# Pairs of row tiles: layer 0's second addition at the pair's end, residues of the four sums on VectorE, residues of the weight differences on GpSimd

## The reference

```
x = x + einsum('bnr,bor->bno', einsum('bni,bri->bnr', x, B[ids0]), A[ids0])
base   = x @ W.T
logits = x @ Wr.T + 5.0 * one_hot(ids1)
gates  = softmax over the top 2 of logits, spread over 8 experts
h      = x @ A1 (8 experts x rank 16)
x = x + base + 2.0 * einsum('bter,bte,eor->bto', h, gates, B1)
```

## Time and profile before

| | us |
|---|---|
| median of 3 runs | 607.76 (602.59 to 610.08) |
| the profiled execution | 612.9 |
| its span, first to last instruction | 611.1 |
| TensorE matmuls busy | 542.6 (89%) |
| VectorE busy | 436.6 (71%) |
| GpSimd busy | 286.4 (47%) |
| ScalarE busy | 273.9 (45%) |
| mean granted TensorE clock, as a share of full | 0.944 |

### The profile page before, as it was taken

One profiled execution on the slowest core, in us unless ns is written; L12 is line 12 of the kernel. 1 busy time (PEld: TensorE's weight loads), 2 busy tenths in 40 slices (PEclk: granted clock), 3 DMA queues, 4 the chain that ended last, 5 costly groups with the idle time before them and its releaser, 6 DMA issues.

```text
span 611.1 us, 9805 instructions
## 1 busy us (share of the span) xinstructions
PE 542.6 (89%) x3356; PEld 479.2 (78%) x3356; DVE 436.6 (71%) x904; ACT 273.9 (45%) x617; POOL 286.4 (47%) x263
## 2 busy tenths in 40 slices
PE   6899999988977889988788897979889798897997
...
GB/s 341 237 103 123 113 112 113 113 113 31 126 69 86 83 107 55 121 86 139 77 66 115 55 139 86 105 95 60 105 86 125 96 39 113 79 103 1 2 92 47
DMA packets 31158, 60.45 MB, mean 99 GB/s; under 512 B 4348, under 2 KB 20476, under 8 KB 31108
## 3 DMA queue, kind: packets, MB, share of 16 engines
...
...
## 4 chain that ended last, share of the span: by engine, by line
PE 42%; DVE 32%; issue 11%; ACT 7%; POOL 5%; DMA 1%; DVEq 1%; POOLq 0%; ACTq 0%
PE o_bank L728 14%; PE o_bank L691 8%; PE x_bank L737 8%; DVE a_raw L1306 5%; PE x_bank L610 5%; DVE weight L1376 4%; DVE xt L1229 3%; DVE xt L1256 3%; ACT bx_pair L934 3%; DVE gate L1380 2%; DVE gate L1383 2%; POOL xs L519 2%; POOL xt L525 2%; PE o_bank L680 2%; DVE b_raw L1298 2%
## 5 line engine op out<-in xcount | busy, mean ns | idle before, releaser
L728 PE MATMUL o_bank<-w_hi,xs 128*128 128x512 f32 x384 | 134.8, 424 | 5.5 <-ACT out_sb L1039 5.3
L536 POOL TENSOR_TENSOR a_t<-a_raw,a_t 64x1024 fp32r<-64x1024 f32 x22 | 52.6, 2389 | 180.2 <-ACT a_t L907 164.0
L728 PEld LDWEIGHTS o_bank<-w_hi,xs 128*128 128x128 f32 x384 | 78.6, 205 | 26.4 <-ACT out_sb L1039 8.7
L691 PE MATMUL o_bank<-w_hi,xs 128*128 128x324 f32 (+1 forms) x336 | 93.5, 352 | 0.0
L728 PE MATMUL o_bank<-w_lo,xs 128*128 128x512 f32 x192 | 80.1, 417 | 0.0
L519 POOL TENSOR_TENSOR xs<-xt,xs 128x512 fp32r<-128x512 f32 x48 | 61.7, 1297 | 38.1 <-ACT xs L991 25.0
L399 POOL DMA_INDIRECT a_in<-in_L_cond_A_dram,a_run x64 | 60.9, 952 | 19.0 <-issue 16.2
L691 PEld LDWEIGHTS o_bank<-w_hi,xs 128*128 128x128 f32 x336 | 62.2, 196 | 5.5 <-issue 1.0
L1306 DVE STREAM_TRANSPOSE a_raw<-a_in 128x1024 f32<-128x1024 f32 x32 | 64.1, 2005 | 3.0 <-DMA a_in<-in_L_cond_A_dram,a_run 3.0
L1184 DVE TENSOR_TENSOR xs<-x_bank,xs 128x512 fp32r<-128x512 f32 x64 | 43.1, 684 | 27.9 <-ACT xt L973 27.4
L1229 DVE STREAM_TRANSPOSE xt<-x_near 128x512 f32<-128x512 f32 x48 | 54.4, 1154 | 9.3 <-POOL xt L525 9.3
...
## 6 DMA issues: line engine op xcount, KB each, us to landing
...
a_in<-in_L_cond_A_dram,a_run POOLq DMA_INDIRECT x64, 3.5
...
```

Source lines behind the costliest of these rows:

```text
L536: nc.gpsimd.tensor_tensor(lower, a_raw[Q:P, m % 2, :], lower.bitcast(F32), ALU.subtract)\
L691: mm = pe.matmul(O[part][:, 0:hi - lo], x1_at(n, c // CB, low)[:, c % CB, :], w[:, c, lo:hi], start=(k == 0), stop=(k == K3 - 1), skip_gro ...
L728: mm = pe.matmul(O[0][:, 0:hi - lo], xs[:, raw_slot(j, c // CB), low, c % CB, :], w[:, c, lo:hi], start=(k == 0), stop=(k == K3 - 1), skip ...
```

## The change

- TensorE: `add_l0(b + 2)` goes from between B2 and `turn_gated` b to the very end of the pair, behind lora b. `make_bx(a + 2)` goes behind lora a, `add_l0(a + 2)` and `make_bx(b + 2)` behind `pair_first_part` b. `turn_gated` a waits for tile a's counts alone.
- VectorE gets the residues of S1 to S4 (`s_lo`) and S4's addition (`make_s4`), which goes to a buffer `s4` of its own, so S2 and the transposes need not wait for each other in the old way. `sums_of_pair` moves from a pair's end to the next pair's start, and the transposes of the next x are spread over the pair in halves.
- GpSimd keeps, in the pairs, A's residue and the gathers. The first `a_lo_paired` waits for the gates of tile a (`gate_step`), the second for the end of a + 2's fold (`bx_step`), and all six gathers come after both. In the single tiles it takes the residues of the weight differences from VectorE (`t_chunk_lo`, m = 6 to 9).
- ScalarE's order follows. Its `t_split` goes one single tile earlier (n = 3 to 6), and the split of b's result goes to the start of the next pair.

```diff
             for m in range(3, K + 2):
...
+                if m >= 6:
+                    t_chunk_lo(m - 6)
+                    pool.wait_ge(t_lo, 2 * (m - 5))
...
             for q in range(PAIRS):
                 a = K + 2 * q
-                s_lo(q, S3, s3_slot(q), xt[:, 0, chunks(0), :])
-                s_lo(q, S2, s2_slot(q), xt[:, 1, chunks(1), :])
-                make_s4(q)
-                if a + 2 < T:
-                    pool.wait_ge(s4_made, q + 1)
-                    a_lo_paired(a + 2, a + 3, a + 3)
-                s_lo(q, S1, s1_slot(q), xt[:, 1, chunks(0), :])
-                s_lo(q, S4, s4_slot(q), xt[:, 1, chunks(1), :])
+                pool.wait_ge(gate_step, GATE * (a + 1))
...
+                if a + 2 < T:
+                    if q == 0:
+                        pool.wait_ge(f_lo, CB)
+                    a_lo_paired(a + 2, a + 3, a + 3)
+                    pool.wait_ge(bx_step, bx_count(a + 3))
+                    a_lo_paired(a + 3, a + 3, a + 3)
                 if a + 4 < T:
                     reload_b(a + 4)
+                    reload_a(a + 4)
                     reload_b(a + 5)
-                    reload_a(a + 4)
-                if a + 2 < T:
-                    pool.wait_ge(ss_lo, 4 * q + S4)
...
-                    a_lo_paired(a + 3, min(a + 5, T - 1), min(a + 4, T - 1))
-                if a + 4 < T:
                     reload_a(a + 5)
...
                 pair_lora(a, 0, O[0])
                 pair_lora(a, 1, PA)
                 if more:
+                    make_bx(a + 2)
+                pair_first_part(q, 1)
+                if more:
+                    add_l0(a + 2)
                     make_bx(b + 2)
-                    add_l0(a + 2)
-                pair_first_part(q, 1)
...
                 product(B2, *w_block(0, 1), PB, False)
-                if more:
-                    add_l0(b + 2)
                 turn_gated(b, bx_count(b + 2) + 1 if more else bx_count(T))
...
                 pair_lora(a, 2, PC)
+                if more:
+                    add_l0(b + 2)
...
-                if K - CB <= n < K:
-                    t_split(n - (K - CB))
+                if 3 <= n < 3 + CB:
+                    t_split(n - 3)
                 out_part(n, 2)
...
+            def make_s4(q):
+                dve.wait_ge(s_step, 3 * q + 3)
+                if q > 0:
+                    dve.wait_ge(ss_lo, 4 * q)
+                nc.vector.tensor_tensor(s4[:, :, :], xt[:, 0, chunks(1), :], xt[:, 1, chunks(1), :],
+                                        ALU.subtract).then_inc(s4_made, 1)
+
+            def s_lo(q, which, slot, raw):
+                dve.wait_ge(ss_hi, 4 * q + which)
+                minus(xs[:, slot, 1, :, :], raw, xs[:, slot, 0, :, :]).then_inc(ss_lo, 1)
+
             def sums_of_pair(q):
                 b = K + 2 * q + 1
                 make_s(q, 1)
                 raw_lo(b, 0)
                 make_s(q, 2)
                 make_s(q, 3)
+                s_lo(q, S3, s3_slot(q), xt[:, 0, chunks(0), :])
+                make_s4(q)
                 raw_lo(b, 1)
+                s_lo(q, S2, s2_slot(q), xt[:, 1, chunks(1), :])
...
+                else:
+                    sums_of_pair(q)
                 if more:
-                    turn_x(a + 2)
                     aT_part(a + 2)
-                    bT_part(a + 2)
                 choose_experts(a)
                 weigh_experts(a)
                 if more:
+                    turn_x_half(a + 2, 0)
+                    bT_part(a + 2)
+                s_lo(q, S1, s1_slot(q), xt[:, 1, chunks(0), :])
+                gated_t_part(a)
+                s_lo(q, S4, s4_slot(q), s4[:, :, :])
+                if more:
+                    turn_x_half(a + 2, 1)
+                    aT_part(b + 2)
+                    bx_half_part(a + 2)
+                    turn_x_half(b + 2, 0)
+                    bx_rest(a + 2)
+                    turn_x_half(b + 2, 1)
                     bT_part(b + 2)
-                    bx_half_part(a + 2)
-                    bx_rest(a + 2)
-                gated_t_part(a)
+                choose_experts(b)
                 if more:
-                    turn_x(b + 2)
+                    raw_lo(a + 2, 0)
+                weigh_experts(b)
+                if more:
+                    raw_lo(a + 2, 1)
                     bx_half_part(b + 2)
-                    raw_lo(a + 2, 0)
                     bx_rest(b + 2)
-                    raw_lo(a + 2, 1)
-                    aT_part(b + 2)
-                choose_experts(b)
-                weigh_experts(b)
                 gated_t_part(b)
-                if more:
-                    sums_of_pair(q + 1)
                 out_b1(q)
                 out_b2(q)
```

97 lines of the change are left out of this document (43 added, 54 removed).

## The result

| | before | after |
|---|---|---|
| median us | 608.92 (4 runs, 602.59 to 612.16) | 568.52 (4 runs, 565.94 to 568.67) |
| profiled execution, its span | 612.9, 611.1 | 565.94, 564.2 |
| setup and tile 0 | 45.27 | 42.93 |
| single tiles 1 to 7 | 123.27 | 124.78 |
| pair 0 | 42.39 | 32.48 |

After over before is 0.9355, 95% interval 0.9293 to 0.9417. The forecast was 565 with 553 to 587. The profiled execution of before is one of its slow ones (612.9, the lowest is 602.59), so the stages of this table add up to 47 us of gain where the medians differ by 40.4.

A forecast was written before the change was run, and what follows sets the result against it. TensorE bounds the kernel, with about 4.8 us of waits a pair, VectorE losing 5.5 behind GpSimd. 612.9 - 42.9 (ten pairs) - 9.8 (pair 0) + 4.5 (single tiles) = 564.7, say 565 us; range 553 to 587.

The forecast's parts named there:

- The waits that are left: TensorE's stops in a new pair: lora a 0.35, make_bx a + 2 0.65, turn_gated b 0.35, lora b 1.2; 2.55 us.
- The mis-sized term: S1's residue on VectorE, at 11.4 us, meets GpSimd's first residue of A and takes 1.2 us in place of 0.6.
- its upper bound for such an operation: A 128x512 VectorE operation held up by GpSimd takes at most 0.6 us plus a whole residue of A, 2.4.
- Ten pairs: Ten pairs of 32.6 us at the full clock: 326 in place of 368.9, -42.9 us.
- a sign of being right: Pairs of 32 to 33 us would show the forecast right; pairs over 34 us would show it wrong.
- Pair 0: 42.39 us become 32.6 if T4's residues fit under the 3.5 us of cover: -9.8 us.
- The sums' front: Sums and residues moved to VectorE's pair start cost nothing, ready 3.5 us before TensorE wants them at S3 and S2.
- The rival with chance 0.19: The clock falls in the new pairs, 1.55 us each over 11 pairs: 17 more, 582 us; chance 0.19.
- VectorE's waits: VectorE keeps its 8.2 us of waits beside 26.2 of work: pairs of 34.4, 585 us; chance 0.17.
- The slower rival: The ring goes on with VectorE's new work added in series: pairs of 39.4, 646 us, deciding from 37.0; chance 0.04.
- The single tiles: ScalarE's earlier t_split delays tiles 5 and 6, 5.5 us lost, 1 back in tiles 6 and 7: +4.5, bounds 0 to 9.
- The waits on `gate_step` and `bx_step`: GpSimd's two waits put both residues of A past VectorE's gates; given as the reason against the 0.04-chance slower case.

The follow-up runs named there:

- Experiment 5: The changed kernel with one more wait: GpSimd's first residue of A in a pair waits for S4's residue on VectorE; 555.93 us, 0.9195.
- experiment 1: The changed kernel without GpSimd's two waits, on gate_step and on bx_step; 568.59 us, 0.9404.
- Experiment 2: The changed kernel with add_l0(b + 2) put back between B2 and turn_gated b; 606.15 us, 0.9995.
- experiment 4: The kernel before with one wait added: GpSimd's first residue of A in a pair waits for the gates of tile a; 599.49 us, 0.9918.
- experiment 8: The changed kernel with ScalarE's t_split back in single tiles 4 to 7 in place of 3 to 6; 562.12 us, 0.9275.

## Why the prediction was right, and where not

**TensorE's own work** was laid out as 32.6 less 2.55 of waits, 30.05. The pair without waits is 30.00.

**The waits that are left** were forecast as 2.55 us at four places. The true price is 33.26 less 30.00, so 3.26. The rows show 0.67, 0.52, 0.29 and 0.94, in sum 2.42. A matmul follows the one before some 0.16 us ahead of that one's modelled end (product S3 in the timeline above: 1.96 long, and S2 starts 1.80 after it). So each stop costs more than its row says, by 0.21 if the 0.84 are shared out evenly (an estimate). With that, lora a is 0.88 (forecast 0.35), `make_bx` a + 2 0.73 (0.65), `turn_gated` b 0.50 (0.35) and lora b 1.15 (1.2).

**The mis-sized term** is S1's residue. The prediction saw that it meets A's residue and gave it 1.2 us in place of 0.6. It took 1.75, and the wait at lora a behind it is the 0.5 that is missing. Experiment 5 shows it: with the meeting gone that wait goes and the pair is 1.08 shorter. Both starting times were right (gates done 9.7 us into the pair against 9.8, A's residue from 10.2 to 12.6 against 10.1 to 12.5). What was wrong is how two such operations share: not a slower rate, but a wait to the end and then most of the length. Behind GpSimd's end the residue has 0.55 of its 0.68 left, the step of 0.35 in experiment 1 has 0.15, and the weight of 0.16 has 0.02. The prediction had read this off the weight, and had put it into its upper bound for such an operation, but not into S1's term. With it the term would have been about 1.7 (11.4 to 12.5, and 0.6). Not all of VectorE's work waits so: the transposes of x, which read one input, take 1.13 to 1.23 us whether they lie beside that GpSimd operation or not. The Trainium skill, "SBUF — State Buffer", section "SBUF: two separate sides", says that the pair of ports that VectorE and GpSimd share is an exclusive lock: a VectorE operation in a 2-port perf mode or with two SBUF inputs (the latter only against a GpSimd operation that reads SBUF), or else the GpSimd operation, whichever starts first, holds it for the whole instruction, and the other blocks. The trace agrees, with 1.75 for the residue, 1.94 for an operation of 0.16 and 2.38 for one of 0.35 in experiment 1.

**Ten pairs**: forecast -42.9, measured -36.3. The 0.66 a pair is this term and the smaller misses beside it. At 33.26 the pairs are just past the 32 to 33 that were named as a sign of being right. **Pair 0**: -9.8 and -9.9, so T4's residues did fit under the cover. **The last pair** kept its length (+0.1). **The sums' front** cost nothing: no wait at product S3 or S2 in any pair. **The gathers** cost nothing.

**The clock** was taken as full in the pairs, and it was. The rival with chance 0.19 fell: four stops of 0.3 to 0.9 a pair and a granted clock of 1.00 throughout. Experiment 2, with one stop of 2.85, shows what can bring it. But a stop that long is not needed. Before, pairs 1 to 4 stayed at the full clock with five stops of 0.5 to 1.5 us, and pairs 5 to 10 had a fall with four of 0.5 to 1.2. In experiment 4 four pairs of ten had one, with stops of 0.5, 1.4 and 0.9. So the size of the longest stop does not decide it, and why the clock held in the new pairs is open: what is shown is that it held in all ten. The Trainium skill, "TensorE: Matmul & The Clock Gate", section "A second HAM failure mode: psum-queue depth-cycling", says that frequent short idles between groups of matmuls make the clock go back and forth. Pairs 5 to 10 of before agree (0.91), the four stops of 0.3 to 0.9 us in each new pair do not (1.00).

**VectorE's waits**, the rival with chance 0.17, came true in part. VectorE is busy for 26.33 us of a pair, where 26.2 was reckoned, and waits for 6.9. The rival had 8.2 and a pair of 34.4, the forecast's pair of 32.6 leaves 6.4 and the measured one is 33.26. **The slower rival** fell: it wanted pairs of 37 us or more.

**The single tiles**: forecast +4.5, measured +1.5, by two misses of opposite sign. Tile 4 lost 6.7 where 5.5 was forecast, by the way described. ScalarE's split waits for GpSimd, and TensorE stops at `turn_gated`:

```profile
92.16 0.83 ACT L1039 CAST t_w<-t_raw 128x324 fp32r<-128x324 f32 x2 [0.89 <-POOL t_raw L493]
...
106.12 0.47 PE L563 MATMUL b_bank<-ident,gated 128*128 128x128 f32 x1 [4.43 <-DVE gated L1389]
```

Tiles 6 and 7 gave back 5.2 where I took 1. What VectorE loses there stood in front of what TensorE waits for. In tile 6 before, two of the eight residues ran from 126.58 to 130.06 us, and the fold's first step, for which ScalarE was done at 127.8, came right behind them, 4.4 us after the tile's start (2.2 in experiment 8, where they are GpSimd's). Experiment 8 shows that the loss in tile 4 has nothing to do with that gain: with `t_split` late again, tile 4 is 16.2 and tiles 6 and 7 together 37.3, against 37.8 after the change and 43.0 before.

**The waits on `gate_step` and `bx_step`** were given as the reason against the slower rival. By experiment 1 the first is idle: ScalarE's order does its work. The conclusion stood on another leg than the one named.

**The total** is near in part by luck, because misses cancel. Between the two profiled executions (564.7 forecast, 565.94 measured) they are +6.6 in the pairs, -3.0 in the single tiles and -2.3 in the setup, whose code is the same. And the forecast starts from an execution of before that is 4 us over its median: -48 was forecast from there, -47 came, and between the medians it is -40.4.
